# Edge chunk of a graph kernel on one core: TensorE's order changed, twelve constant products added

## What is computed

```python
h = relu(layernorm(x))
ea = edge_attr @ W_edge.T + b_edge
msg = relu(h[src] + ea)
aggr = segment_sum(msg, dst, N_NODES)
x = x + relu(((1 + eps) * h + aggr) @ W1.T + b1) @ W2.T + b2
h = relu(layernorm(x))
m = relu(h[src]) + 1e-7
a = exp(m - seg_max[dst]) / denom[dst]          # softmax over the edges of a destination
x = x + (h + segment_sum(a * m, dst)) @ W + b
```

## Time and profile before

| | |
|---|---|
| median of 3 runs | 3434.68 us (3431.54 to 3447.72) |
| profiled execution, its own time | 3426.78 us |
| its span, first to last instruction | 3424.9 us |
| mean granted clock of TensorE | 0.752 |
| busy share PE, DVE, ACT, POOL | 59%, 55%, 22%, 50% |
| matmuls of the edge products (L644), mean | 3136, 354 ns |
| matmuls of the counts (L760), mean | 2352, 409 ns |
| matmuls of the sums (L631), mean | 3120, 293 ns |
| gathers of the first layer (L563), mean | 1563, 953 ns |

### The profile page before, as it was taken

One profiled execution on the slowest core, in us unless ns is written; L12 is line 12 of the kernel. 1 busy time (PEld: TensorE's weight loads), 2 busy tenths in 40 slices (PEclk: granted clock), 3 DMA queues, 4 the chain that ended last, 5 costly groups with the idle time before them and its releaser, 6 DMA issues.

```text
span 3424.9 us, 44898 instructions
## 1 busy us (share of the span) xinstructions
PE 2010.0 (59%) x11221; PEld 1599.4 (47%) x11222; DVE 1894.2 (55%) x4523; ACT 762.6 (22%) x1322; POOL 1727.2 (50%) x1820
## 2 busy tenths in 40 slices
PE   2454555555555555655565655565655575577778
PEld 1244444444454444444454544454544464355546
DVE  7555565556565556565565655565656784233233
ACT  4000011111122222232233333333333443000000
POOL 5355555555555555555555555555555402444441
PEclk8677777777777777777777777777777786788888
DMA  4022223223333333333333333333222217455453
GB/s 127 19 56 63 66 67 81 71 72 82 80 80 80 83 85 88 89 96 96 93 94 93 106 98 97 94 103 81 68 59 55 53 31 248 132 164 168 157 178 113
DMA packets 152069, 322.51 MB, mean 94 GB/s; under 512 B 65291, under 2 KB 106027, under 8 KB 137791
## 3 DMA queue, kind: packets, MB, share of 16 engines
q1 hardware_dynamic: 27286, 151.94, 15.0%
q0 software_dynamic: 61632, 100.73, 12.9%
q10 hardware_dynamic: 63014, 68.51, 5.8%
HBM read 247.64 MB, written 73.38 MB: 94 GB/s over the span
## 4 chain that ended last, share of the span: by engine, by line
another core or an unknown queue 26%; PE 23%; DVE 22%; issue 17%; DVEq 5%; ACT 1%; DMA 0%; SPq 0%; ACTq 0%
DVE zone L1354 11%; PE ps L834 10%; PE ps L760 5%; DVE planes L1125 5%; DVE ps L1326 4%; PE ps L644 4%; PE ps L631 2%; DVEq L1354 2%; PE ps L844 1%; DVEq L373 1%; DVE planes L1131 1%; PE ps L665 1%; DVE features_buf L1339 1%; DVE onehot L1125 1%
## 5 line engine op out<-in xcount | busy, mean ns | idle before, releaser
L563 POOL DMA_INDIRECT rows_buf<-table,index x1563 | 1489.9, 953 | 1207.3 <-DVE ps L1326 734.0
L760 PE MATMUL ps<-zone,planes 128*128 128x400 f16 x2352 | 682.4, 409 | 1138.6 <-DVE zone L1354 770.6
L760 PEld LDWEIGHTS ps<-zone,planes 128*128 128x128 f16 x2352 | 266.8, 114 | 1329.6 <-issue 1271.3
L977 ACT ACTIVATE features_buf<-ps 128x800 f16<-128x800 f32 x392 | 328.0, 837 | 1953.8 <-remote 931.5
L1354 DVE TENSOR_SCALAR zone<-iota_c,planes 128x400 f16<-128x400 int16 x2352 | 654.9, 332 | 57.1 <-issue 45.1
L644 PEld LDWEIGHTS ps<-wet,zone 128*128 128x128 f32 x3136 | 617.7, 276 | 51.0 <-issue 46.8
L644 PE MATMUL ps<-wet,zone 128*128 128x96 f32 x3136 | 592.0, 354 | 0.0
L1326 DVE TENSOR_TENSOR ps<-ps,rows_buf 128x768 f32<-128x768 f32 x195 | 188.1, 965 | 552.5 <-remote 512.4
L1125 DVE TENSOR_TENSOR onehot<-ps,dstf 128x1024 f32<-128x1024 f32 x196 | 237.6, 1212 | 456.1 <-remote 441.4
L631 PE MATMUL ps<-onehot,features_buf 128*96 128x128 f32 x3120 | 453.0, 293 | 3.2 <-issue 3.2
L631 PEld LDWEIGHTS ps<-onehot,features_buf 128*96 128x96 f32 x3120 | 419.3, 182 | 17.9 <-issue 5.5
(11 more groups left out here) (184 smaller groups left out, 780.7 us busy)
## 6 DMA issues: line engine op xcount, KB each, us to landing
zone<-edge_t SPq DMA_DIRECT2D x98, 768.0 KB
counts<-features_buf ACTq DMA_DIRECT2D x288, 200.0 KB
rows_buf<-counts SPq DMA_DIRECT2D x24, 1600.0 KB
rows_buf<-table,index POOLq DMA_INDIRECT x1563
planes<-counts SPq DMA_DIRECT2D x12, 1600.0 KB
table<-planes SPq DMA_DIRECT2D x5, 840.0 KB
final<-residual ACTq DMA_DIRECT2D x48, 48.0 KB
out<-final ACTq DMA_DIRECT2D x48, 48.0 KB
```

Of the source, the lines that this page charges most:

```text
L563: nc.gpsimd.indirect_dma_start(out=into[:, t, :], out_offset=None, in_=table, in_offset=bass.IndirectOffsetOnAxis(ap=at[:, t:t + 1], axis= ...
L760: nc.tensor.matmul(count_ps[:, bass.ds(banks[k], WC)], row_hot[:, u % 2, g * GS + k, :], pair_hot[:, g * GS + k, :], start=False, stop=Fal ...
L977: nc.scalar.activation(count_out[:, k], bank, ACT.Copy, accum_out=row_sum[:, bass.ds(p, 1)]).then_inc(moved, 1)
```

## The change

In a chunk, all waits now stand ahead of the first matmul; the order becomes edge products half 0, count group 0, six products of constants, group 1, half 1, groups 2 and 3, six products of constants, all eight sums. `more_sums` (a branch that these data take only where a chunk spans over 128 destinations) follows. The constants' results go to unused columns of the PSUM bank that the chunk's sums use, and nobody reads them.

```diff
+            def keep_busy(u, n, start=True):
+                for k in range(n):
+                    nc.tensor.matmul(ps[:, 2 + u % 2, 3 * WIN:4 * WIN], ones[:, :], ident[:, :], start=start,
+                                     stop=True, skip_group_check=not start)
+
             def chunk(i, u, ends=False):
                 c = i * NS + u
                 v = (u + 1) % NS
                 steps, more_at = steps_of(c)
                 pe.wait_ge(row_done, c + 1)
-                count_steps(c, u, 0, *steps[0])
+                pe.wait_ge(onehot_done, c + 1)
+                pe.wait_ge(acc_done, c + 1)
                 pe.wait_ge(msg_done, c + 1)
                 pe.wait_ge(edges_in[v // 2], (i + (1 if v else 2)) * 16)
                 edge_linear(v, 0)
+                count_steps(c, u, 0, *steps[0])
+                keep_busy(u, 6)
                 count_steps(c, u, 1, *steps[1])
                 edge_linear(v, 1).then_inc(ea_done, 1)
-                pe.wait_ge(onehot_done, c + 1)
-                pe.wait_ge(acc_done, c + 1)
-                sums(0, u, sum_ps[u % 2], onehot[:, u % 2], range(0, TH))
                 count_steps(c, u, 2, *steps[2])
-                sums(0, u, sum_ps[u % 2], onehot[:, u % 2], range(TH, T)).then_inc(sum_done, 1)
+                count_steps(c, u, 3, *steps[3])
+                keep_busy(u, 6)
+                sums(0, u, sum_ps[u % 2], onehot[:, u % 2]).then_inc(sum_done, 1)
+                more_sums(0, u, *more_at)
                 if ends:
-                    more_sums(0, u, *more_at)
                     last_sums(c + 1, u + 1)
-                count_steps(c, u, 3, *steps[3])
-                if not ends:
-                    more_sums(0, u, *more_at)
```

## The result

The changed kernel takes **3667.1 us** (median of 4, 3662.2 to 3673.8) against 3438.8 for the kernel before (median of 4): a ratio of 1.066, with a 95% interval of 1.063 to 1.070, 228 us slower. The profiled execution took 3673.8 us, its span is 3671.9 (3424.9 before), so the spans differ by 247 us.

The account below looks back on a forecast made before the run. Bound: a loop in which gather bursts hold back TensorE's completions. Terms 258 + 77 + 36 + 12 - 55 = +328 us on the profiled 3426.8 gave 3755, as median 3763, said as 3760; range 3320 to 3990 (own 3480 to 3990).

Parts of the forecast that it names:

- doubles: Edge-loop chunks whose sum_done waits for two gather bursts in a row: half of the 30 turn plain, 55 us less.
- The lock loop: In the edge loop, TensorE's completions come out mostly when POOL's gather burst has landed; add to add takes 13.2 us.
- The clock gives nothing back: In the edge loop, granted clock rises to about 0.85, but waits end with the burst: counted at nothing with gathers.
- The chunk behind ACT: Group 3, now ahead of the sums, waits for ACT's cleared pair in 89 chunks; sum_done 6.3 us after ea_done.
- Slips: Chunks whose sum_done falls +4 us or more into the next burst and waits it out: 50 plus 15, 5.15 us each.
- Group 1 on group 0: In 18 chunks group 1, before ea_done, needs a pair ending in group 0; half of them delay ea_done: 36 us.
- The last eight chunks: Chunks without gathers have little TensorE idle time, so the twelve constant products cost 1.5 us each, 12 us.
- late one-hots: Sign in the profile: DVE's waits before the one-hot of L1125 that name 'remote', 30 before, 60 to 90 forecast.
- (a): Faster rival: completions get out in lulls of a burst, no slips, all 30 doubles gone, 3336 us; chance 0.20.
- (b): Faster rival: warm TensorE completes before the burst is dense, chunk at POOL's pace of 9.9 us, 2806 us; chance 0.06.
- (c): No-change rival: the added work lies in idle time, slips don't occur, doubles stay, 3447 us; chance 0.10.
- (d): Much slower rival: every chunk slips, sum_done coming later than about 4 us after the add, 4310 us; chance 0.09.

Follow-up runs that it names:

- few_before_d: Kernel before with one gather a chunk in place of eight: 2407.9 us against 3448.1, 0.698 (chip 3); the same on chip 6: 2206.1 us, 0.896.
- order_only_c: Changed kernel without its twelve constant products, so the new order alone, on chip 11: 3488.3 us against 3443.9 for the kernel before, 1.014.
- constants_only_c: Kernel before with twelve constant products between ea_done and the sums, nothing moved, on chip 11: 3484.4 us against 3443.9, 1.012.
- group3_last_d: Changed kernel with count group 3 put back behind the sums, constants kept, on chip 3: 3448.8 us against 3448.1 for the kernel before, 1.002.

## Why the prediction came out as it did

The time was to be 3760 and is 3667, inside the forecast's own range (3480 to 3990), on the side that had 0.64. The mechanism is the forecast's, though not all of its terms are, and two errors of the term for doubles cancel, which is luck. Step by step:

- **The lock loop** (TensorE's completions held while gathers fly). Right, shown by few_before_d (0.698) and the count above. That it belongs to some chips only was nowhere in the prediction; no trace of one chip could have told.
- **The clock gives nothing back.** Right: 0.75 to 0.85 and slower; on chip 11 the order alone has 0.77 and 1.014, the constants alone 0.86 and 1.012. The Trainium skill's page "TensorE: Matmul & The Clock Gate", section "Why this matters for your kernels", advises to keep TensorE busy for throughput; these traces agree on the clock and not on the time: even where nothing is held, 0.86 became 0.97 with the constants alone and the kernel 1.3% slower, as gathers set the pace.
- **The chunk behind ACT.** A wait for ACT's cleared ahead of the sums was the right cause, but the prediction has it for group 3 alone. The trace has 43 such waits ahead of group 2 beside 39 ahead of group 3, and of the 45 chunks over 16.5 us 28 have one at group 2 (17 only there) and 20 one at group 3 (9 only there). What changed for group 2 is a move that the prediction names but prices for group 1 alone: half 0 went ahead of group 0. Group 0's last product was drawn as over 2.9 us into a burst (median), and now 5.9. order_only_c has this move and 26 waits for ACT ahead of group 2; constants_only_c, without it, has 4. Counted from dst by the prediction's rule, group 2 needs a pair that ends in group 0 of its chunk 59 times and in group 1 12 times; 35 of the 43 waits are of the first sort. (The same count has 69 chunks for group 3 on group 1, 16 on group 0 and 7 on group 2, near the prediction's 82 and 7.) Even so the place of group 3 decides: group3_last_d takes the loss away. The forecast's 6.3 us from ea_done to sum_done stands on the timeline as 1581.25 - 1573.86 = 7.4 after the add, with the six constants at 2.59 us rather than 1.6.
- **Slips: 65 x 5.15 = 335 us.** Too many, and a little too dear: 45 chunks of 18.18 us against 13.64 for a plain one, 4.5 each, 204 us, and 19 more of 2.0 each, 39 us. Together 243. The assumption "from +4 on" was fair (2 to 5 by the count), but of the 77 chunks with such a pair group 3 waited in 39 only, and group 2's waits, for which there was no term, made up for a part.
- **Group 1 on group 0: 36 us** for some chunks. Measured: the plain chunk itself is 0.41 us longer, 68 us over 167 chunks, twice the term. Part of that may be the constants' (13.46 in constants_only_c, 13.23 before), part stays unassigned.
- **Doubles: -55 us, half of them gone.** All are gone. By the distances they cost before 29 x (20.88 - 13.23) - 52 x (13.23 - 10.18) = 63 us, and that is what was given back. That is 2.2 us for each of the 29, where the prediction has 3.7 (111 for all thirty): the price was too high and their going underrated, and that 55 comes near 63 is luck. The reason given, more products ahead of ea_done, isn't what did it: constants_only_c has none there, and only 3 of its chunks take over 20 us. The runs tie it to the sums' place between bursts; why ea_done itself no longer gets out inside a burst there (0 of 138, against 9 of 128 before) stays open.
- **The last eight chunks: 12 us.** Behind the last gather (2723.6 and 2956.8 us) the spans run on for 701.3 and 715.1, 14 us more. The last seven adds there are 10.9 us apart on the mean and were 9.2 (the 8.8 of the earlier trace rows is from two of these distances; others are up to 10.0), so a chunk costs 1.7 and not 1.5. Two of them:

```profile
3007.31 0.97 DVE L1330 TENSOR_TENSOR ps<-ps,rows_buf 128x768 f32<-128x768 f32 x1 [1.00 <-PE ps L644]
3018.33 0.97 DVE L1330 TENSOR_TENSOR ps<-ps,rows_buf 128x768 f32<-128x768 f32 x1 [0.94 <-PE ps L644]
```

The terms measured, 243 + 68 - 63 + 14 = 262, against 247 us between the spans; they leave out the first 400 us, where the changed kernel gained some 8 us, and its two chunks under 12.5 us, which give another 5. What was to be seen was seen: adds 15.05 us apart (15.5 forecast), 69 late one-hots (60 to 90), clock 0.85, and POOL's wait for the add up by 251 us, about what was lost. What the prediction lacks altogether is that a chip may hold nothing. Of the rivals, (a) had the right idea on doubles and fell on the slips; (b) and (c) fell with them, and (d) needed three times as many slips.

## What to carry to other kernels

When several engines are let go in the same instant and the trace names nobody, look at what ended just then on an engine that none of them waits for; where it is a burst of gathers, place each handshake against the burst, not against the engine's own work, and follow every wait that stands ahead of a signal, also those whose producer was moved. Holding the next burst back until the sums were out (gate) was worth 6.3%; filling idle time with work ahead of that signal cost 5 to 6.6% with a wait for ACT ahead of it too, and 1.2% without. And time the kernel before on more than one chip: the order alone cost 0 on one and 1.4% on another, one gather in place of eight gave 10% and 30%.

## What the runs showed of the hardware that I had not expected

The same program takes 2460 us on two chips (6 and 14) and 3431 to 3448 on three (7, 11 and 3), 40% more, steady to within about 1% on each. (The chip of the pair in the result isn't on record; its kernel before takes 3438.8.) The gathers are issued no slower (0.95 to 0.97 us on the mean on either). What is later is their landing, as the page has it with one gather a chunk (few_before_d on chip 3, then few_before on chip 6; the last number is the median in us from issue to landing):

```profile
rows_buf<-table,index POOLq DMA_INDIRECT x196, 3.7
```

```profile
rows_buf<-table,index POOLq DMA_INDIRECT x196, 2.6
```

Their last packets end 1.3 us (median) after the end of the issue on both, so it is again the signal that is later, by 1.1 us. With full bursts, on the slower chips TensorE's completions, and its taking up of further work, mostly stand still from some 2 to 5 us after a burst of gathers begins until 2 us or so after its last issue. Why the chips differ no run here shows.
